# Masked attention in a new order of engine work, with masks as 64x64 tiles and transposes woven into projections

## The reference

```
x = x + attention1(layernorm(x), ctx, ctx)            # no mask
x = x + expert_ffn(layernorm(x))
# attention of the second layer
energy = einsum('nqhd,nkhd->nhqk', q, k)
energy = where(mask == 0, -1e20, energy)
attn   = softmax(energy / sqrt(256), axis=3)
x = x + einsum('nhql,nlhd->nqhd', attn, v).reshape(...) @ Wo.T + bo
x = x + spiking_ffn(layernorm(x))
```

## Time and profile before

| | |
|---|---|
| time, median of 3 runs | 3880.64 us (3880.34 to 3881.94) |
| profiled execution, first to last instruction | 3869.9 us |
| its own time by the whole-program clock | not listed apart; the runs lie 10.4 to 12.0 us above the span |
| busy in the span | PE 95%, PEld 74%, DVE 80%, ACT 57%, POOL 57% |
| mean granted TensorE clock | 0.981 of 2.4 GHz |
| masked attention, first to last store of maxima | 2419.5 to 3152.8 us |

### The profile page before, as it was taken

The page is one execution under the profiler, slowest core; times in us unless marked ns, Lnnn a source line. Parts: engine busy times, 40 slices in busy tenths (PEclk is TensorE's granted clock), DMA queues, the critical chain, the costliest instruction groups (busy, mean ns, idle before and its releaser), DMA issues. The chain is left out here.

```text
span 3869.9 us, 134428 instructions
## 1 busy us (share of the span) xinstructions
PE 3678.2 (95%) x47408; PEld 2870.0 (74%) x47408; DVE 3088.5 (80%) x5266; ACT 2207.4 (57%) x4529; POOL 2200.5 (57%) x3316
## 2 busy tenths in 40 slices
PE   5999999995799999999999996999999999999999
PEld 4777777773688888888888884566666668888888
DVE  4888888885778777778777775798888977777777
ACT  3777777775444444444444442577677765555554
POOL 5666666664245443333333334466666667887777
PEclk9999999997899999999999998899999999999999
DMA  4677777774332322222222224799999952232322
GB/s 130 197 204 207 214 209 209 205 213 154 102 85 79 84 68 74 66 70 69 68 72 68 72 66 90 158 211 216 211 217 208 215 151 80 75 77 75 79 75 72
DMA packets 834241, 502.59 MB, mean 130 GB/s; under 512 B 262037, under 2 KB 824408, under 8 KB 833480
## 3 DMA queue, kind: packets, MB, share of 16 engines
q1 hardware_dynamic: 832680, 493.49, 50.5%
q0 software_dynamic: 928, 0.49, 0.1%
HBM read 251.27 MB, written 214.96 MB: 120 GB/s over the span
## 5 line engine op out<-in xcount | busy, mean ns | idle before, releaser
L1556 ACT ACTIVATE phase_spare<-phase_loop_hid,phase_b1T 128x128 f32<-128x128 f32 x2048 | 586.1, 368 | 710.9 <-PE phase_loop_hid L193 702.2
L1129 DVE TENSOR_REDUCE phase_loop_mx<-phase_loop_score 128x8 f32<-128x1024 f32 x512 | 625.4, 1222 | 98.5 <-PE phase_loop_score L882 91.0
L1522 PE MATMUL phase_loop_moe_y<-phase_w,phase_spare 128*128 x2048 | 693.6, 379 | 0.1
L1037 ACT ACTIVATE phase_loop_pt<-phase_loop_scoreT 128x1024 f32<-128x1024 f32 x448 | 458.6, 1024 | 268.3 <-PE phase_loop_scoreT L916 265.8
L1524 PE MATMUL phase_loop_moe_y<-phase_w,phase_spare 128*128 x2048 | 558.2, 273 | 0.0
L191 PE MATMUL phase_loop_hid<-phase_loop_moe_h,all_w_first_hi 128*128 128x128 f16 x2048 | 449.2, 219 | 0.0
L192 PE MATMUL phase_loop_hid<-phase_loop_moe_h,all_w_first_hi 128*128 128x128 f16 x2048 | 449.1, 219 | 0.0
L192 PE MATMUL phase_loop_hid<-phase_loop_moe_h,phase_w_hi 128*128 128x128 f16 x2048 | 449.1, 219 | 0.0
L193 PE MATMUL phase_loop_hid<-phase_loop_moe_h,all_w_first_lo 128*128 128x128 f16 x2048 | 449.1, 219 | 0.0
L193 PE MATMUL phase_loop_hid<-phase_loop_moe_h,phase_w_lo 128*128 128x128 f16 x2048 | 449.1, 219 | 0.0
L191 PE MATMUL phase_loop_hid<-phase_loop_moe_h,phase_w_hi 128*128 128x128 f16 x2048 | 449.0, 219 | 0.0
(11 more groups left out here) (293 smaller groups left out, 11038.9 us busy)
## 6 DMA issues: line engine op xcount, KB each, us to landing
qk_scratch<-phase_loop_qk SPq DMA_DIRECT2D x192, 256.0 KB, 3.4
phase_loop_cin<-in_ctx SPq DMA_DIRECT2D x128, 256.0 KB, 4.6
x_scratch<-phase_loop_x SPq DMA_DIRECT2D x128, 256.0 KB, 3.1
h_scratch<-phase_loop_hr SPq DMA_DIRECT2D x128, 256.0 KB, 3.7
phase_loop_qS<-qk_scratch SPq DMA_DIRECT2D x384, 64.0 KB, 2.8
phase_loop_kS<-qk_scratch SPq DMA_DIRECT2D x384, 64.0 KB, 2.4
ks_scratch<-ct_scratch SPq DMA_DIRECT2D x384, 64.0 KB, 2.4
all_w_first_lo<-ks_scratch SPq DMA_DIRECT2D x128, 192.0 KB, 4.0
```

Of the source, the lines that this page charges most:

```text
L1037: act.activation(pt[n % len(pt)][:, :, :], score_t_bank[:, :].rearrange("p (j n) -> p j n", j=HB2), ACT.Exp, scale=exp_scale).then_inc(s_e ...
L1129: v.tensor_reduce(to, score_bank[:, :].rearrange("p (h j n) -> p h j n", h=2, j=CH), AX.X, ALU.max).then_inc(s_mx.sem, 1)
L1522: pe.matmul(o[:, :], hh[n % NH][:, j, :], row, start=half == 0 and j == 0, stop=False, skip_group_check=True)
L1556: i = act.activation(hf[n % NF][:, j, :], hid(u, n)[:, j * S:(j + 1) * S], ACT.Gelu, bias=w["b1"][:, bass.ds(e * HB + (4 * half + j), 1)], ...
```

## The change

All of it is in the masked attention, its preparation and its hand-over to the spiking part.

- Masks: `mask_tiles` writes a mask with four products of 64x64 tiles of the identity and 512 columns, in place of two products of 128x128. Two of them need the mask with its halves of rows exchanged (`mask_x`, `maskT_x`), which POOL makes with four DMAs while the weights are prepared.
- Which group is masked where: n = 0 by Relu, exponential and product on ACT and POOL; n = 1, 2, 3 by mask products on PE. The minimum on DVE is gone.
- The lists of all engines are written anew; on PE the tasks that use the array in one way stand together.
- `braid` puts single transposes between the products of a projection: the four of `y1` among the twelve of `o`, the eight of `y0` and `t_y` among the six of `q`. A wait of a woven task is met at its first transpose.
- `t_y` has a PSUM bank of its own (`ring3[0]`), which the spiking part takes over once `lo_y` of the last unit is done.
- The first attention's PE list is the same in another notation (`whole`).

```
-CUT_BY_MIN, CUT_BY_PRODUCT = (1,), (3,)
+CUT_BY_PRODUCT = (0,)
...
+def braid(count, main, places, *sides):
+    def go(s):
+        def part(lag, task):
+            return task(Unit(0, s - lag)) if 0 <= s - lag < count else iter(())
+        between = chain.from_iterable(part(*side) for side in sides)
+        for i, _ in enumerate(part(*main)):
+            for _ in range(places.count(i)):
+                next(between, None)
+        for _ in between:
+            pass
+    return None, go
...
-            plan = [(8, "t_y"), (4, "t_max"), (1, "q"), (7, "y1"), (6, "y0"), (8, "o")]
-            shared = ((), ("t_max", "q", "o"), ("t_y", "y1", "y0"))
+            plan = [(4, "t_max"), (7, "o"), (6, "y1"), (1, "q"), (5, "y0"), (6, "t_y")]
+            shared = (("t_y",), ("t_max", "o", "q"), ("y1", "y0"))
...
-                    tasks = [(5, load_c), (1, load_xT), (5, store_max), (3, stack_q), (11, store_x1), (12, store_h),
-                             (2, store_q), (8, load_r), (5, place_max), (2, stack_k)]
+                    tasks = [(2, store_q), (3, load_c), (2, stack_k), (4, store_max), (0, load_xT), (2, stack_q),
+                             (6, load_r), (4, place_max), (7, store_x1), (9, store_h)]
...
-                    tasks = [(11, rows1), (4, maxima), (5, ctx_as_v), (6, cut(p, 3)), (9, rstd1)]
+                    tasks = [(9, rows1), (5, cut(p, 0)), (8, rstd1), (4, ctx_as_v), (3, maxima)]
...
+                def mask_tiles(bank, rows, crossed):
+                    for b, part in enumerate((rows, crossed)):
+                        for i in range(2):
+                            k_at, out_at = slice(64 * i, 64 * i + 64), slice(64 * (i ^ b), 64 * (i ^ b) + 64)
+                            pe.matmul(bank[out_at, b * 512:(b + 1) * 512], c["identb"][k_at, k_at], part[k_at, :],
+                                      start=True, stop=False, skip_group_check=True)
...
-                    tasks = [(6, av(0)), (3, score(0)), (8, make["t_y"]), (5, mask_score_t(0)), (4, make["t_max"]),
-                             (5, score_t(0)), (3, mask_score(1)), (6, av(1)), (3, score(1)), (5, score_t(1)),
-                             (1, make["q"]), (7, make["y1"]), (3, mask_score(2)), (5, mask_score_t(2)), (3, score(2)),
-                             (6, av(2)), (5, score_t(2)), (6, av(3)), (3, mask_score(3)), (6, make["y0"]),
-                             (3, score(3)), (5, score_t(3)), (8, make["o"]), (2, mask_score(0))]
+                    tasks = [(3, mask_score(0)), (3, score(0)), (5, score_t(0)), (6, av(2)), (6, av(3)),
+                             (4, whole(make["t_max"])),
+                             (3, mask_score(1)), (5, mask_score_t(1)), (3, score(1)), (5, score_t(1)),
+                             braid(units, (7, make["o"]), (2, 3, 4, 5), (6, make["y1"])),
+                             (3, mask_score(2)), (5, mask_score_t(2)), (3, score(2)), (5, score_t(2)),
+                             (5, av(0)), (5, av(1)),
+                             (3, mask_score(3)), (5, mask_score_t(3)), (3, score(3)), (5, score_t(3)),
+                             braid(units, (1, make["q"]), (0, 1, 2, 3, 4, 4, 5, 5), (5, make["y0"]), (6, make["t_y"]))]
...
-                    tasks = [(5, copy_max), (6, expo(0)), (6, expo(1)), (2, hi_q), (7, copy_y(0)), (6, expo(2)),
-                             (7, copy_y(1)), (10, norm1), (6, expo(3)), (6, expo_under(3)), (8, hi_y)]
+                    tasks = [(5, expo(0)), (5, expo_under(0)), (4, copy_max), (6, copy_y(1)), (5, expo(1)), (5, expo(2)),
+                             (8, norm1), (5, copy_y(0)), (5, expo(3)), (1, hi_q), (6, hi_y)]
...
-                    tasks = [(8, norm_y(0)), (10, add_x), (4, row_max(0)), (10, norm1_stats), (9, lo_y),
-                             (4, row_max(1)), (8, norm_y(1)), (2, lo_q), (4, row_max(2)), (6, cut(v, 1)),
-                             (4, row_max(3))]
+                    tasks = [(2, lo_q), (3, row_max(0)), (7, lo_y), (8, norm1_stats), (3, row_max(1)), (6, norm_y(1)),
+                             (7, add_x), (3, row_max(2)), (3, row_max(3)), (5, norm_y(0))]
...
+        g.wait_ge(s_v, 1 + CH)
+        cross(w["mask_x"], w["mask"])
+        g.wait_ge(s_turned, CH)
+        cross(w["maskT_x"], w["maskT"])
+        g.wait_ge(s_cross, 64)
...
-                    if u.no == 1:
-                        before["sums"].wait(pe, ended)
+                    if u.no < 2:
+                        before[("turned", "sums")[u.no]].wait(pe, ended)
```

More of the change, by code:

```diff
@@ L21 @@
 from contextlib import ExitStack
+from itertools import chain
 import numpy as np
@@ L127, in step @@
         for lag, task in tasks:
-            if 0 <= s - lag < count:
+            if lag is None:
+                task(s)
+            elif 0 <= s - lag < count:
                 task(Unit(0, s - lag))
@@ L193, in three_passes, with passes, whole, go @@
     return eng.matmul(out, l_lo, r_hi, start=False, stop=stop)
+def passes(eng, out, l_hi, l_lo, r_hi, r_lo, start, stop, done=None):
+    yield eng.matmul(out, l_hi, r_hi, start=start, stop=False)
+    yield eng.matmul(out, l_hi, r_lo, start=False, stop=False)
+    m = eng.matmul(out, l_lo, r_hi, start=False, stop=stop)
+    if done:
+        m.then_inc(done.sem, 1)
+    yield m
+def whole(part):
+    def go(u):
+        for _ in part(u):
+            pass
+    return go
+def braid(count, main, places, *sides):
[7 more added lines that the diff above has]
+        for _ in between:
+            pass
+    return None, go
 def together(nc, *programs):
@@ L566, in attention @@
         more = then and then(k, half_banks(score_bank) + half_banks(score_t_bank), [ring3[0], av_bank], pt, {
-            "scores": s_mx, "weights": s_e, "products": s_av, "sums": s_ye, "h": d_h, "x": d_x1, "late": s_late})
+            "scores": s_mx, "weights": s_e, "products": s_av, "sums": s_ye, "turned": s_yl, "h": d_h, "x": d_x1, "late": s_late})
         def follow(engine, eng):
@@ L812, in t_x @@
                     free("t_x", u)
-                    transpose_pair(pe, ring["t_x"], ln0.xn[u.slot], ident).then_inc(s_tx.sem, 1)
+                    yield from transpose_pair(pe, ring["t_x"], ln0.xn[u.slot], ident, s_tx)
                 def t_c(u):
@@ L817, in t_c, with project @@
                     free("t_c", u)
-                    transpose_pair(pe, ring["t_c"], cin[u.slot], ident).then_inc(s_tc.sem, 1)
-                def project(u, bank, src, name, bias, ones):
+                    yield from transpose_pair(pe, ring["t_c"], cin[u.slot], ident, s_tc)
+                def project(u, bank, src, name, bias, ones, done):
                     hi, lo = w[name]
@@ L857, in q @@
                     free("q", u)
-                    project(u, ring["q"], lambda u: xT[u.slot], "wq", "bq", c["ones10"]).then_inc(s_q.sem, 1)
+                    yield from project(u, ring["q"], lambda u: xT[u.slot], "wq", "bq", c["ones10"], s_q)
                 def kk(u):
@@ L862, in kk @@
                     free("k", u)
-                    project(u, ring["k"], lambda u: cT[u.slot4], "wk", "bk", c["ones6"]).then_inc(s_k.sem, 1)
+                    yield from project(u, ring["k"], lambda u: cT[u.slot4], "wk", "bk", c["ones6"], s_k)
                 def vv(u):
@@ L867, in vv @@
                     free("v", u)
-                    project_rows(u, ring["v"], lambda u: cT[u.slot4], "wv").then_inc(s_v.sem, 1)
+                    yield from project_rows(u, ring["v"], lambda u: cT[u.slot4], "wv", s_v)
                 def score(n):
@@ L890, in go @@
                         s_mx.wait(pe, u, n)
-                        for hh in range(2):
-                            pe.matmul(score_bank[:, hh * 512:(hh + 1) * 512], c["identb"][:, :], w["mask"][:, :], start=True,
-                                      stop=False, skip_group_check=True)
+                        mask_tiles(score_bank, w["mask"], w["mask_x"])
                     return go
@@ L924, in go @@
                         s_e.wait(pe, u, n)
-                        for hh in range(2):
-                            pe.matmul(score_t_bank[:, hh * 512:(hh + 1) * 512], c["identb"][:, :], w["maskT"][:, :],
-                                      start=True, stop=False, skip_group_check=True)
+                        mask_tiles(score_t_bank, w["maskT"], w["maskT_x"])
                     return go
@@ L965, in t_y @@
                     free("t_y", u)
-                    transpose_pair(pe, ring["t_y"], yn[u.slot], ident).then_inc(s_y2.sem, 1)
+                    yield from transpose_pair(pe, ring["t_y"], yn[u.slot], ident, s_y2)
                 def o(u):
```

70 lines of the change are left out of this document (37 added, 33 removed).

## The result

The changed kernel takes 3925.5 us (median of 4 runs, 3921.2 to 3932.5) against 3880.5 for the kernel before (4 runs): a ratio of 1.0121, 95% interval 1.0104 to 1.0138, so it is slower by 1.2%. Forecast were 3936 us and slower. The profiled execution has a span of 3919.4 us, 49.5 more than the profiled one before; the medians differ by 45.0.

The account below looks back on a forecast made before the run. A loop of the maxima through ACT, SP and PE was to bind: 3.04 + 5.26 + 0.7 + 3.6 = 12.6 us a unit against 11.64. Over 63 units +60, less 5, on span 3869.9, plus 10.7: 3936 us, range 3865 to 3982.

Parts of the forecast that it names:

- The ring of the maxima: Masked attention, score_t(0) through store_max and place_max to the next score_t(0): 12.6 us a unit, binding; chance 0.62.
- stretch: SP's list from store_max to place_max: some issues take longer than usual, 0.7 us a unit, bounds 0 and 1.1.
- the short loop: Rival in the masked attention: maxima land in 2.5 us, the loop binds at 11.5 us, 3867 us; chance 0.13.
- The sum: Whole kernel: (12.6 - 11.64) x 63 = +60, less 5, on the span 3869.9, plus 10.7 around it: 3936 us.
- the shorter pipeline: PE's pipeline, one step shorter (largest lag 7, not 8): 0 to 10 us less, taken as 5.
- The 10.7 us "around" the span: Whole kernel: amount added to the forecast span to get the median, as the two stood before.
- What SP does behind place_max is hidden: SP's list after place_max (store_x1 to stack_k): some 2.7 us, covered because store_max returns only 3.6 + 3.04 us later.
- PE's sum of 9.7 us: PE's work per masked attention unit after the change: 9.7 us, between 8.7 and 11.8, not binding.
- the fast rival: Masked attention: place_max lands before PE needs it (landing plus stretch below 3.3 us), PE binds, 3817 us; chance 0.15.
- The falling clock: Rival on PE: idle stretches lower its granted clock, 13.3 us a unit, 3981 us; chance 0.10.
- DVE, ACT and POOL do not bind: Masked attention: DVE loses 1.69 us a unit from about 10.4, ACT and POOL keep their work; none binds.

Follow-up runs that it names:

- e3: The changed kernel with copy_max moved ahead of expo_under(0) on ACT and load_xT ahead of store_max on SP: 3910.0 us, ratio 1.0089 to the kernel before.
- e6: The changed kernel with PE computing q of unit s, not s-1, at the end of its step: 3912.8 us, ratio 1.0098 to the kernel before.
- e5: e3 with PE also computing q of unit s, not s-1, at the end of its step: 3858.7 us, ratio 0.9958 to the kernel before.
- e4: The kernel before with only its masks changed, to four products of 64x64 tiles: 3871.4 us, ratio 0.9994.
- e10: e5 with the stores of x1 and h issued from ACT's list instead of SP's: 3858.1 us, ratio 0.9960 to the kernel before.

## Why the prediction was right

**The ring of the maxima: right, and slightly too long.** Forecast 12.6 us, found 12.46 in the mean and 11.90 in the turn shown. Over 54 turns its steps are 6.03 us for 5.96 (5.26 of issues and 0.7 of stretch), 3.43 for 3.6, and 3.11 for 3.04. The stretch of issues was real: load_xT took 2.06 us in the turn shown for 1.25. The Trainium skill's fixed 2.0 us (DMA: Bandwidth & Descriptors, Anatomy of one DMA) is below the median that both kernels show (4.1 and 3.2), and the short loop that would follow from it did not come. The section gives the figure for DMAs that GpSimd issues, and these are issued by SyncE, so the comparison is a loose one.

**The sum: right.** (12.6 - 11.64) x 63 = 60 was 51.7; the shorter pipeline was to give 5 and the rest of the span gives 2.2. The 10.7 us "around" the span are no cost of the program: every run that lists its own span is 1.8 us longer than it, and the profiled execution before was a quick one. The forecast took them as an offset between profile and median, which leaves the difference of 55 us untouched. The median is 10.5 us below the forecast.

**What SP does behind place_max is hidden: wrong.** This is the step that failed. The prediction set SP's work there (some 2.7 us) against the 6.6 us until the next store_max, and priced no wait in it. store_q at the head of SP's list waits for lo_q in 24 of 31 units. The prediction followed one value, the maxima, and declared the rest of the list covered. Following q in the same way (q last in PE's step, store_q first in SP's, stack_q and its landing ahead of score(0)) would have given a second ring of 24 us over two units. It is why the time does not depend on either ring alone, and why PE's idle time stands in two places, 21.4 us at score_t(0) and 18.3 at score(0), and not as 2 us at score_t(0) in every unit. That the forecast of the time still holds is luck in part: the ring that was not priced holds the unit at 12.37 us by itself (e3) and the one that was at 12.35 (e6). Had it been longer, each microsecond a unit would have added 63.

**PE's sum of 9.7 us: too short by 1.4.** The masks (0.24 for 0.22) and the switches (0.07 to 0.10 for 0.09) were right. The two braids were priced at 3.0 us (2.0 for 18 products, 1.0 for 12 transposes) and are 4.2; the rest is 6.9 for 6.7. A transpose woven in costs as much as a product, and not something between 0.03 and its old price. Since PE does not bind, this cost nothing here; for the fast rival it counts.

**The fast rival: its condition and its time were both wrong.** It was to come if the landing and stretch fell under 3.3 us, at 3817 us. In e3 the ring, where nothing else holds it, takes 4.71 us from store to place_max, 3.89 to score_t(0) and 2.14 to the next store, so 10.7, well under the 11.6 at which that condition stands, and the time is 3910. With both rings open it is 3859, and 3840 with 11% less traffic: PE's step is 11.1 us and not 9.7.

**The falling clock: a part of it.** The granted clock in the two windows is 0.97 and 0.96 where it had been 1.00, and again 1.00 in e5, whose waits are short. It did not lead to the long case of 3981 us. Its share is small: of the 54 turns between 2450 and 3140 us, 35 ran at a granted clock of 0.99 or more and took 12.44 us in the mean, 15 ran below 0.95 and took 12.90, and all together 12.56. So it cost about 0.1 us a unit.

**DVE, ACT and POOL do not bind: right.** DVE went from 268.5 to 215.0 busy us of 300, with no gain from it.

## What to carry to other kernels

When tasks are given another order and other lags, follow every value that leaves the engines and comes back (here q as well as the maxima), add up each ring, and divide by the number of units over which it closes. Two rings of nearly one length hide each other: loosening either seems worthless (0.2% and 0.3% here, hardly beyond the noise), loosening both gave 1.6%, so an experiment that gains little and moves a wait to a new place is not yet a refutation. An engine that is 99% busy may still be relieved for nothing, as e4 shows (296.49 of 300 us before); ask what the next bound is before shortening its work.

## What was not expected of the hardware

- Four 64x64 tiles, two of which write each bank from different rows of the array, run side by side: 0.24 us a mask for 0.44.
- A 128x128 transpose of 32-bit data between two f16 products takes 0.11 us, as they do; four in a row 0.12 to 0.13 each. Weaving does not hide it.
- Landings lengthen with the load, the issuing does not visibly: with the DMA share at 1.13 in e5's first window the median from the issue to the landing is 4.8 us, with 0.83 in the kernel after 3.2. stack_q's six issues take 2.73 us, or 3.67 (kernel after) and 4.27 (e5) at times, but their mean between 2570 and 2962 us is 3.67 us a unit in the kernel after and 3.61 in e5.
- One microsecond of issues a unit moved from SP's queue to ScalarE's changed nothing (e10 against e5).
